# Summing softmax exponentials in two steps: GpSimd adds the halves, VectorE sums the smaller tile (layers zero and one)

## The reference, cut to what matters

```
logits = einsum('bhnk,bmk->bhnm', q, k) / sqrt(16)     # 77 keys
logits = where(causal, logits, -inf)                   # layer one only
attn   = softmax(logits, axis=-1)
out    = einsum('bhnm,bmv->bhnv', attn, v)
```

## Time and profile before

| | |
|---|---|
| median of 3 runs | 3016.26 us (3013.68 to 3017.59) |
| profiled execution, its own time | 3026.86 us |
| its span, first to last instruction | 3025.1 us |
| mean granted TensorE clock | 0.901 of full speed |
| DVE busy | 1959.8 us (65%) |
| PE busy | 2458.2 us (81%) |
| ACT busy | 1507.4 us (50%) |
| POOL busy | 790.0 us (26%) |

### The profile page before, as it was taken

The page is one execution under the profiler, slowest core; times in us unless marked ns, Lnnn a source line. Parts: engine busy times, 40 slices in busy tenths (PEclk is TensorE's granted clock), DMA queues, the critical chain, the costliest instruction groups (busy, mean ns, idle before and its releaser), DMA issues. The chain is left out here.

```text
span 3025.1 us, 43676 instructions
## 1 busy us (share of the span) xinstructions
PE 2458.2 (81%) x16566; PEld 1994.3 (66%) x16566; DVE 1959.8 (65%) x4449; ACT 1507.4 (50%) x2566; POOL 790.0 (26%) x699
## 2 busy tenths in 40 slices
PE   4778888876488999999848999999998386868665
PEld 2545555554377888888648999999998254545444
DVE  2487878885555666666535656666664458686867
ACT  1356666664445655565424544444553254545433
POOL 1133434332222434444440000000000562525020
PEclk8678888986799999999879999999999698989888
DMA  7400000000000111100014334433431510201000
GB/s 259 176 1 1 16 15 15 8 8 8 31 15 1 38 36 39 36 14 23 19 35 158 120 115 133 136 116 122 142 121 65 155 52 28 66 29 57 1 15 14
DMA packets 152616, 184.22 MB, mean 61 GB/s; under 512 B 21560, under 2 KB 118101, under 8 KB 152408
## 3 DMA queue, kind: packets, MB, share of 16 engines
q1 hardware_dynamic: 140120, 154.29, 15.5%
q0 software_dynamic: 12288, 27.15, 2.9%
HBM read 116.38 MB, written 71.43 MB: 62 GB/s over the span
## 5 line engine op out<-in xcount | busy, mean ns | idle before, releaser
L2343 POOL DMA_INDIRECT picked<-expert_out,so x128 | 126.3, 987 | 867.7 <-DMA so<-slots 764.9
L157 PE MATMUL SC<-Xhi,Whi 128*128 128x320 f32 x1024 | 320.4, 313 | 7.1 <-DVE Wlo L2136 5.3
L157 PE MATMUL SC<-Xlo,Whi 128*128 128x320 f32 x1024 | 317.4, 310 | 0.0
L157 PE MATMUL SC<-Xhi,Wlo 128*128 128x320 f32 x1024 | 317.4, 310 | 0.0
L621 POOL TENSOR_TENSOR PR<-PR,rs 128x616 f32<-128x616 f32 x128 | 157.6, 1231 | 421.8 <-DVE rs L1002 421.6
L1372 POOL TENSOR_TENSOR ff_Hlo<-ff_HF,ff_Hhi 128x512 fp32r<-128x512 f32 x112 | 147.9, 1321 | 425.6 <-ACT ff_Hhi L1505 425.5
L157 PEld LDWEIGHTS SC<-Xhi,Whi 128*128 128x128 f32 x1024 | 193.4, 189 | 7.8 <-DVE Wlo L2136 5.7
L2113 ACT ACTIVATE Hhi<-HF 128x320 fp32r<-128x320 f32 x256 | 120.6, 471 | 154.7 <-DVE HF L2166 154.7
L157 PEld LDWEIGHTS SC<-Xlo,Whi 128*128 128x128 f32 x1024 | 193.5, 189 | 0.0
L157 PEld LDWEIGHTS SC<-Xhi,Wlo 128*128 128x128 f32 x1024 | 193.1, 189 | 0.0
L2155 DVE TENSOR_TENSOR Hlo<-HF,Hhi 128x320 fp32r<-128x320 f32 x256 | 125.4, 490 | 104.2 <-ACT Hhi L2113 104.2
(11 more groups left out here) (478 smaller groups left out, 7015.6 us busy)
## 6 DMA issues: line engine op xcount, KB each, us to landing
expert_in<-zeros SPq DMA_DIRECT2D x4, 5120.0 KB, 32.3
rowsin<-expert_in SPq DMA_DIRECT2D x32, 640.0 KB, 6.1
expert_out<-rowsout SPq DMA_DIRECT2D x32, 640.0 KB, 4.0
Wraw<-L_wg SPq DMA_DIRECT2D x32, 512.0 KB, 7.1
Wraw<-L_wu SPq DMA_DIRECT2D x32, 512.0 KB, 7.3
Wraw<-L_wd SPq DMA_DIRECT2D x32, 512.0 KB, 8.0
X<-x SPq DMA_DIRECT2D x8, 512.0 KB, 3.8
x_after_l_attention<-X SPq DMA_DIRECT2D x8, 512.0 KB, 2.8
```

What stands on the lines that cost most here:

```text
L157: last = nc.tensor.matmul(out, lhs[l], rhs[r], start=start and n == 0, stop=stop and n == 2)
L2343: nc.gpsimd.indirect_dma_start(picked[g][:, t, k, :], None, oute[:, :], bass.IndirectOffsetOnAxis(ap=so[g][:, t, k:k + 1], axis=0)).then_i ...
```

## The change

GpSimd gets a new operation for each unit, `fold(n)`: it adds columns 0 to 39 of each head's 80 to columns 40 to 79 and writes the 128 x 8 x 40 sums to one of two new tiles. VectorE's `sums(n)` then waits for `folded` and not for `probs`, and reduces the 8 x 40 tile. In GpSimd's list `fold` of the unit that starts in a step stands behind `normalise` of the unit before, and ahead of everything else in that step. `fold(n)` waits for `probs` of unit n and, from unit 2 on, for `rsum` of unit n - 2 (the tile it overwrites).

```diff
+        folds = two("fold", [P, HH, CTXP // 2])
...
+                    def fold(n):
+                        pool.wait_ge(probs, n + 1)
+                        if n >= 2:
+                            pool.wait_ge(rsum, n - 1)
+                        pr = PR[n % NPA]
+                        nc.gpsimd.tensor_tensor(folds[n % 2][:, :, :], pr[:, :, 0:CTXP // 2], pr[:, :, CTXP // 2:], add).then_inc(folded, 1)
+
...
-                            n = UNIT_AT.get((h + 1) * PERIOD + s - 1)
+                            now, n = (UNIT_AT.get((h + 1) * PERIOD + s - d) for d in range(2))
                             if n is not None:
                                 normalise(n)
+                            if now is not None:
+                                fold(now)
...
                     def sums(n):
-                        dve.wait_ge(probs, n + 1)
+                        dve.wait_ge(folded, n + 1)
                         r = rs[n % NPA]
-                        link(nc.vector.reduce_sum(r[:, :], PR[n % NPA][:, :, 0:CTX], AX))
+                        link(nc.vector.reduce_sum(r[:, :], folds[n % 2][:, :, :], AX))
                         nc.vector.reciprocal(r[:, :], r[:, :]).then_inc(rsum, 1)
```

More of the change, by code:

```diff
@@ L554, in attention_layers @@
             sm_all = Sems(nc, rnd)
-            (scores_ready, shifted, probs, rsum, pnorm, pt_psum, pt_ready, ot_psum, ot_ready, vchain, ctx_in,
+            (scores_ready, shifted, probs, folded, rsum, pnorm, pt_psum, pt_ready, ot_psum, ot_ready, vchain, ctx_in,
              var_p, sd_p, rstd_p, xn_p, xt_p_psum, xt_p, q0_psum, q0_ready,
@@ L562, in attention_layers @@
                 sm_all.one("t_" + n) for n in (
-                    "scores_ready", "shifted", "probs", "rsum", "pnorm", "pt_psum", "pt_ready", "ot_psum", "ot_ready", "vchain", "ctx_in",
+                    "scores_ready", "shifted", "probs", "folded", "rsum", "pnorm", "pt_psum", "pt_ready", "ot_psum", "ot_ready", "vchain", "ctx_in",
                     "var_p", "sd_p", "rstd_p", "xn_p", "xt_p_psum", "xt_p", "q0_psum", "q0_ready",
```

## The result

The changed kernel is slower by 0.4%: 3029.81 us median of 8 runs (3027.77 to 3035.39) against 3017.60 us for the kernel before, run on the same chip (8 runs, 3012.31 to 3027.92). The ratio is 1.0039 with a 95% interval of 1.0025 to 1.0053. In a second series it was 3033.6 against 3016.19 us, 1.0044 (1.0024 to 1.0063). The forecast was 3023 us, within 3006 to 3035, and leaned to slower.

What follows compares the result with a forecast made beforehand. DVE was taken to set the pace in steps 2 to 9, elsewhere waits for other engines. -16.3 + 15.3 + 3.0 + 1.0 + 3.4 = +6.4 us on the median 3016.3 us gave 3023 us, range 3006 to 3035.

Steps and rivals of the forecast that it cites:

- The saving: Each unit's sum over 320 elements, not 616: 0.298 us less per unit, 16.3 us removed, mostly in steps 2 to 9.
- The hold: Short DVE operations beside a fold in steps 2, 3, 4, 7 and 8 are held by it: 15.3 us added.
- So there it is in time: In the steps that set the pace, the fold is done before DVE wants it, behind the next shift.
- The spline addition: Step 14's fold pushes POOL's spline addition back 0.6 us in about five of eight halves: 3.0 us added.
- The ends: Late folds in the last units' bursts and drains, 3.4 us, and at units 7 and 8, 1.0 us.
- The clock of the drain: A PE clock that moves with the changed pauses, listed among what would make the forecast wrong, without a size.
- No contention: Rival 1: short DVE operations run free beside the fold, the rest stands; -8.9 us, 3007 us; chance 0.18.
- All savings count: Rival 2: DVE is the bound in every step and waits move along; -38 us, 2978 us; chance 0.04.
- The fold as slow as normalisation: Rival 3: each fold takes 1.23 us, contention 25 us; +21 us, 3037 us; chance 0.13.
- Nothing: Rival 4: reduction price or held operations off by a third, near-equal sums cancel; 3013 to 3020 us; chance 0.17.

Runs made afterwards that it cites:

- the short sum alone: Kernel before, without a fold, DVE's sum over only the first 40 of each head's columns (320 elements); ratio 0.9981 (0.9964 to 0.9998).
- the write-only kernel: Changed kernel with a GpSimd memset of about the same duration in place of the fold, sum of exponentials left out; 3024.29 against 3012.89 us for before.
- the kernel that isolates the drains: Changed kernel with folds in units 112 to 127 only, all others summed whole; 3019.78 against 3016.34 us for before, ratio 1.0012.
- the pair: One profile of each kernel, no further edit, each with its own time near its median: before 3014.30 us, changed 3029.38 us.
- the unused fold: Changed kernel whose fold nobody reads; DVE waits for the exponentials and sums all 77 columns; 3045.41 against 3012.89 us for before.

## Why the prediction came out right, and where its sum was wrong

**The saving.** 0.298 us per unit forecast, 0.305 measured; 16.3 us of it on the path, 13.8 measured in the steady part by the short sum alone (12.0 at like clock). That half of it dies ahead of ACT's roots was right.

**The hold.** 15.3 us forecast, 16.9 us measured (50.2 against 33.3 us held), against a fold of 0.88 us forecast and 0.865 measured. The price of L1040 in step 2 was 0.60 us (0.62 forecast), of L1030 in step 3 0.55 us (0.46), as the fold beside it ended 0.2 us late; the operation ahead of L1030, which ran until 0.3 us after the fold's start, is the likely reason. In step 8 it wasn't L1017 but the scalar operation two places on that the fold met, as the exponentials came late there; the price was 0.65 and not 0.43 us. By step, 2 to 4 grew by 9.8 us (11.9 forecast), 7 and 8 by 5.3 us (3.4), and step 13 by 1.9 us, which had no term. So the places of the first are as forecast, and the good fit of the total is in part luck: in step 7 it is mostly the bias addition, met because the sum comes late, that holds DVE (5.4 us against 1.0 and 1.6 before) and not a fold. That reads of GpSimd hold DVE's two-input operations, as the Trainium skill says (SBUF — State Buffer, "Who interferes with whom"), is shown by the write-only kernel: 0.19 us beside a memset, 0.79 beside a fold. The same section of the Trainium skill has `tensor_scalar` among the operations that can contend as well, in what it calls the 2-port modes. The 1.65 us of L1083 agree; whether it ran in such a mode no run shows.

**The step that failed** is "So there it is in time". DVE waited for the fold in 27 units, 15.2 us, of which 12.0 us in the steady part (10.8 in the second profile). I had worked with a normalisation that starts right at `rsum` and with exponentials that are there by then. In 14 units the exponentials came late, in 11 of them right behind a table load of ACT, and the fold's 0.86 us then stands bare in front of the sum (6.7 us). In step 6 of every second half POOL is behind with the keys and values of layer one (2.9 us). Semaphores made POOL's backlog, which had been harmless, DVE's. The kernel without step 6's folds got 6.3 us back by its profile, about 1.6 us at like clock. The steady part was forecast at about +2 us (-16.3 + 15.3 + 3.0) and measured at +11.3, of which about 3 us are low-clock halves. Measured in the same way as a change between before and after: DVE busy for 9.6 us less (saving and holds together), waits for the fold +11.4, for ACT's roots +4.8, for PE's scores +2.6, for the spline addition +1.4; the rest are small waits.

**The spline addition** was forecast at 3.0 us more waiting in the steady part; the wait grew by 2.2 us between 170 and 760 us, and by 1.4 us (5.8 to 7.2) in the steady part itself.

**The ends.** Bursts and start, 4.4 us forecast: 1.5 us in the kernel that isolates the drains, 0.5 us in the changed one, and 0.3 us at the start. Late folds there lie beside waits for PE's scores.

**The clock of the drain**, +4 us, had no term at all; the prediction named it only as a way to be wrong. With it the parts of the table add up: the forecast sum was +6.4 us, the traces of the pair have +15.1, the medians +12.2 and +17.4. The measured time is inside the range in part by luck: what the sum lacked, 9 us in the steady part and 4 us in the drain, was met by 3 to 4 us too much at the ends.

**The rivals.** No contention: falls with the unused fold. All savings count: falls with the short sum. The fold as slow as normalisation: 0.865 us, falls; the time it gave, 3037 us, is about as near to the first median (3029.81) as the forecast is, and nearer to the second (3033.6), but its terms aren't those measured. Nothing: falls, as both intervals lie above 1.

## What to carry to other kernels

An operation moved to GpSimd is priced by what VectorE does beside it, not by GpSimd's idle share: each short VectorE operation with two inputs in SBUF that started beside such a read here ended with it. And a new wait turns the other engine's lateness into one's own, so look at the helping engine where its list is fullest and where its input comes late, not at its mean. Where whole-kernel times scatter by 0.3% with the same code, compare a stretch between two fixed instructions over two profiles of each kernel, and look at TensorE's granted clock inside it before giving a difference of a few us to an edit.

## What the runs showed of the hardware that was not expected

- A GpSimd instruction can be held in turn: folds beside VectorE's 128x1024 multiplication (1.2 us) took 1.94 us twice where 0.86 is usual, when the two had started within 3 ns of each other (fold from 524.14 to 526.07, multiplication from 524.14 to 525.35 us). The multiplication kept its usual time.
- A GpSimd memset left VectorE's operations with two inputs in SBUF alone (none of 57 held) and held a scalar operation with one: L1083 took 1.65 us beside a normalisation and a memset in a row, 0.20 when alone.
- TensorE's granted clock in one and the same stretch was 1.00 of full speed in one kernel and 0.50 in another, where the work ahead had moved by a few us, and this cost 4 us where nothing else covered PE. In the steady part it differed even between two profiles of the same code: four matmuls took 605 ns each in one and 1075 ns in the other, and the half was 1.7 us longer.
